# A layer norm's reciprocal root by ScalarE's square root, a reciprocal and one Newton step, in a Macaron block of two expert layers around a Mamba layer

## The reference

```python
x = x + 0.5 * ffn(layernorm(x))     # 64 experts, top 3, hidden 512, capacity 64 per expert
x = x + mamba(layernorm(x))         # projection, 4-tap convolution, selective scan over 16 states
x = x + 0.5 * ffn(layernorm(x))

def layernorm(x, eps=1e-5):
    m, v = mean(x), var(x)
    return (x - m) / sqrt(v + eps)
```

## Time and profile before

| | us |
|---|---|
| timed runs (three) | 800.65, 801.97, 798.1 |
| median | 800.65 |
| span of the profiled execution, first to last instruction | 795.9 |
| device time of the profiled execution | not among the times shown |
| TensorE busy in the span | 685.0 (86%) |
| VectorE busy | 607.8 (76%), 1042 instructions |
| ScalarE busy | 442.2 (56%), 925 instructions |
| GpSimd busy | 490.3 (62%) |

### The profile page before, as it was taken

One profiled execution on the slowest core, in us unless ns is written; L12 is line 12 of the kernel. 1 busy time (PEld: TensorE's weight loads), 2 busy tenths in 40 slices (PEclk: granted clock), 3 DMA queues, 4 the chain that ended last, 5 costly groups with the idle time before them and its releaser, 6 DMA issues. The chain is left out here.

```text
span 795.9 us, 27862 instructions
## 1 busy us (share of the span) xinstructions
PE 685.0 (86%) x11782; PEld 420.8 (53%) x11782; DVE 607.8 (76%) x1042; ACT 442.2 (56%) x925; POOL 490.3 (62%) x308
## 2 busy tenths in 40 slices
PE   6539999978968999899998989999989439999957
PEld 2524556548644445464554655464546334556547
DVE  7993555536698999899999999989897974555525
ACT  2301555534678878888897997867523102444420
POOL 3004666520248999989999999999961005666520
PEclk8858999999969999999999999999996758999979
DMA  8997998626354441344445143542008805998538
GB/s 275 397 327 211 376 371 301 195 75 262 92 125 109 124 122 36 104 108 138 108 123 120 45 129 78 138 108 57 3 3 293 342 1 168 363 382 276 167 121 318
DMA packets 86087, 141.08 MB, mean 177 GB/s; under 512 B 8340, under 2 KB 33566, under 8 KB 84689
## 3 DMA queue, kind: packets, MB, share of 16 engines
q1 hardware_dynamic: 81552, 126.99, 51.0%
q0 software_dynamic: 4416, 12.39, 4.3%
HBM read 112.02 MB, written 27.57 MB: 175 GB/s over the span
## 5 line engine op out<-in xcount | busy, mean ns | idle before, releaser
L1343 POOL TENSOR_TENSOR BIG<-BIG,R 128x1024 f32<-128x1024 f32 x127 | 305.6, 2435 | 18.5 <-DVE BIG L1266 13.8
L1266 DVE TENSOR_TENSOR_SCAN BIG<-BIG,ps 128x1024 f32<-128x1024 f32 x128 | 285.9, 2270 | 18.4 <-PE ps L896 17.7
L896 PE MATMUL ps<-BIG,stack 64*32 64x128 f32 x8192 | 153.7, 281 | 26.4 <-DVE BIG L1266 21.7
L896 PEld LDWEIGHTS ps<-BIG,stack 64*32 64x32 f32 x8192 | 118.5, 108 | 99.1 <-DVE BIG L1266 66.8
L741 POOL DMA_INDIRECT R<-xn_dram,tok_idx x64 | 65.2, 1019 | 91.1 <-DVE row_idx L674 71.3
L755 POOL DMA_INDIRECT y_dram<-BIG,row_idx x64 | 64.7, 1010 | 64.5 <-DVE BIG L698 57.0
L683 DVE COPY BIG<-ps 128x512 f32<-128x512 f32 x64 | 44.3, 691 | 70.3 <-PE ps L518 70.3
L390 ACT ACTIVATE BIG<-BIG 128x512 f32<-128x512 f32 x64 | 40.4, 631 | 97.1 <-DVE BIG L690 97.1
L1140 ACT ACTIVATE BIG<-R,An 128x510 f32<-128x510 f32 x128 | 84.1, 708 | 5.0 <-DVE BIG L1266 4.9
L1140 ACT ACTIVATE BIG<-BIG,An 128x510 f32<-128x510 f32 x128 | 83.7, 708 | 0.2
L918 PE MATMUL ps<-BIG,fold 128*32 128x512 f32 x512 | 68.8, 611 | 0.0
(11 more groups left out here) (173 smaller groups left out, 1018.9 us busy)
## 6 DMA issues: line engine op xcount, KB each, us to landing
BIG<-in_L_ffn_w SPq DMA_DIRECT2D x120, 512.0 KB, 5.8
BIG<-y_dram SPq DMA_DIRECT2D x18, 512.0 KB, 9.3
BIG<-dt_dram SPq DMA_DIRECT2D x32, 256.0 KB, 4.2
R<-c_dram SPq DMA_DIRECT2D x32, 256.0 KB, 7.2
R<-dt_dram SPq DMA_DIRECT2D x32, 256.0 KB, 5.0
y_dram<-zeros SPq DMA_DIRECT2D x3, 2048.0 KB, 16.2
y_dram<-zeros SPq DMA_DIRECT2D x6, 1024.0 KB, 8.3
xn_dram<-R POOLq DMA_DIRECT2D x2, 2048.0 KB, 11.2
```

The costliest lines, as they stand in the source:

```text
L896: last = nc.tensor.matmul(ps[CW * slot:CW * slot + CW, 2 * (st % 2) + b, :] .rearrange("p (g s k) -> p k g s", g=2, k=4)[:, k], dT[q % 2][ ...
L1266: nc.vector.tensor_tensor_scan(state[st % 3], dA[:, st % 6].rearrange("p b g t -> p (b g t)"), ps[:, u:u + 2, :].rearrange("p b n -> p (b ...
L1343: nc.gpsimd.tensor_tensor(prod[st % RP], state[st % 3].rearrange("p (b g t) -> p b g t", b=2, g=2), Cf[q % 2][:, 2 * gp:2 * gp + 2].rearra ...
```

## The change

The four places outside the scan (first expert stage, tiles 0 to 3 and 4 to 7 of the Mamba stage, second expert stage) get `root_vector` and `root_scalar` in place of `inverse_root`: VectorE adds eps, ScalarE takes the square root, VectorE the reciprocal, and one Newton step and nmr follow. So rstd is raised six times, not thirteen, and a new semaphore, root, tells VectorE that the square root is there. The 24 tiles ahead of the scan keep the old way, since ScalarE's table is another one there. In ScalarE's queue the second square root of the Mamba stage stands between normalise(0) and xt_copy(0). The square root's table set is loaded by hand at ScalarE's start, at the start of the Mamba stage and ahead of the last x_copy. To have a semaphore left for root, b2's transfer is counted on w2's semaphore, and mm2's wait for b2 goes into the one for w2.

```diff
--- before.py
+++ after.py
@@ -90,7 +90,8 @@
-STAT_TOTALS = dict(stats=NI, meanvar=NI, rstd=13)
+STAT_TOTALS = dict(stats=NI, meanvar=NI, rstd=6, root=1)
+NEWTON = 13
 LN_TOTALS = dict(normed=24, normed_act=8, transposed=8, xT=8)
 MOE_TOTALS = dict(logits=5, m8=NI, ix8=NI, ixf=1, mdiff=1, gexp=1, gs=3, V=K, marks=2, mask=2, before=1, running=1,
                   prefix=4, picked=7, W=K, place=K, halves=1, gathered_codes=3, code=1, decode=8, xn_stored=16,
@@ -256,6 +257,29 @@
             step(nc.vector.scalar_tensor_tensor(out=nmr[:, i0:i1], in0=mv[:, i0:i1, 0], scalar=-1.0, in1=r,
                                                 op0=ALU.mult, op1=ALU.mult))
+        def root_vector(e, S, i0, i1, n, m):
+
+            def step(instruction):
+                nonlocal n
+                n += 1
+                instruction.then_inc(S("rstd"), 1)
+                e.wait_ge(*S.at("rstd", n))
+
+            v, y, z, r = rs[:, 0, i0:i1], rs[:, 1, i0:i1], rs[:, 2, i0:i1], rstd[:, i0:i1]
+            step(nc.vector.tensor_scalar(v, mv[:, i0:i1, 1], EPS, None, ALU.add))
+            e.wait_ge(*S.at("root", m + 1))
+            step(nc.vector.reciprocal(r, z))
+            step(nc.vector.tensor_tensor(y, r, r, ALU.mult))
+            step(nc.vector.scalar_tensor_tensor(out=z, in0=y, scalar=-0.5, in1=v, op0=ALU.mult, op1=ALU.mult))
+            step(nc.vector.scalar_tensor_tensor(out=r, in0=z, scalar=1.5, in1=r, op0=ALU.add, op1=ALU.mult))
+            step(nc.vector.scalar_tensor_tensor(out=nmr[:, i0:i1], in0=mv[:, i0:i1, 0], scalar=-1.0, in1=r,
+                                                op0=ALU.mult, op1=ALU.mult))
+
+        def root_scalar(e, S, i0, i1, n):
+
+            e.wait_ge(*S.at("rstd", n + 1))
+            nc.scalar.activation(rs[:, 2, i0:i1], rs[:, 0, i0:i1], ACT.Sqrt).then_inc(S("root"), 1)
+
         def ln_stats(e, S, g0, g1, before_stats=None):
             for g in range(g0, g1 + 1):
                 for i in range(4 * g, 4 * g + 4) if g < g1 else ():
@@ -269,7 +293,7 @@
         def ln_vector(e, S, g0, before_stats=None):
             ln_stats(e, S, g0, 8, before_stats)
             e.wait_ge(*S.at("meanvar", NI))
-            inverse_root(e, S, 0, NI, 0)
+            root_vector(e, S, 0, NI, 0, 0)
         def ln_normalise(e, S):
             for i in range(NI):
@@ -279,6 +303,7 @@
         def ln_scalar(e, S, ST):
+            root_scalar(e, ST, 0, NI, 0)
             e.wait_ge(*ST.at("rstd", STAT_TOTALS["rstd"]))
             for i in range(3, NI, 4):
                 nc.scalar.activation(XN[:, i, :], X[:, i, :], ACT.Identity, bias=nmr[:, i:i + 1],
@@ -309,7 +334,7 @@
                 b = RING + EARLY.index(s)
                 return b, G(f"{name}_{b}"), 16 * (f + 1)
             loads = ROUNDS - (s in EARLY)
-            return s, G(f"{name}_{s}"), 16 * (loads * f + r + 1)
+            return s, G(f"{name}_{s}"), 16 * (loads * f + r + 1) + (16 * (ROUNDS * f + r + 1) if name == "w2" else 0)
         def moe_sync(e, S, f):
             def load_w1(r, s):
@@ -323,7 +348,7 @@
                             w2v[bass.ds(RING * r + s, 1)].rearrange("o p a h -> (o p) a h")).then_inc(loaded, 16)
             def load_b2(r, s):
-                e.dma_start(b2s[s], b2v[bass.ds(RING * r + s, 1)].rearrange("o w a d -> (o w) a d")).then_inc(G(f"b2_{s}"), 16)
+                e.dma_start(b2s[s], b2v[bass.ds(RING * r + s, 1)].rearrange("o w a d -> (o w) a d")).then_inc(G(f"w2_{s}"), 16)
             def reload_w1(j, s, r):
@@ -533,9 +558,10 @@
                 e.wait_ge(*S.at("hT", j + 1))
                 b, loaded, count = weights("w2", f, r, s)
                 e.wait_ge(loaded, count)
+                if b != s:
+                    e.wait_ge(G(f"w2_{s}"), 16 * (2 * ROUNDS - 1) * (f + 1))
                 if later(j):
                     e.wait_ge(*S.at("yo", j - 1))
-                e.wait_ge(G(f"b2_{s}"), 16 * (ROUNDS * f + r + 1))
                 for a in range(2):
                     nc.tensor.matmul(ps[a * CAP:(a + 1) * CAP, 5 + s % 2, 0:D], ones[0:3, 0:CAP], b2s[s][:, a, :],
                                      start=True, stop=False)
@@ -1041,7 +1067,7 @@
             def normalise(q):
                 wait(e, "t_psum", q)
                 if q < 3:
-                    wait(e, "rstd", STAT_TOTALS["rstd"] * (q + 1))
+                    wait(e, "rstd", (6, 12, 12 + NEWTON)[q])
                 for j in range(4):
                     i = 4 * q + j
                     last = nc.scalar.activation(XNc[:, j, :], X[:, i, :], ACT.Identity, bias=nmr[:, i:i + 1],
@@ -1142,7 +1168,10 @@
                 last.then_inc(M("dA"), 1)
             e.wait_ge(M("pads"), 3)
+            nc.scalar.preload_act_table_set("sqrt_and_others")
+            root_scalar(e, MST, 0, 4, 0)
             normalise(0)
+            root_scalar(e, MST, 4, 8, 6)
             xt_copy(0)
             normalise(1)
             raw_copy(0, 0)
@@ -1279,10 +1309,12 @@
             moe_sum(e, F[0], 0)
             stats(0, 4)
-            statistics(0, 4, 0)
+            wait(e, "meanvar", 4)
+            root_vector(e, MST, 0, 4, 0, 0)
             moe_sum(e, F[0], 1)
             stats(4, 8)
-            statistics(4, 8, STAT_TOTALS["rstd"])
+            wait(e, "meanvar", 8)
+            root_vector(e, MST, 4, 8, 6, 1)
             moe_sum(e, F[0], 2)
             for m in range(6):
                 tap(0, m // 3, m % 3)
@@ -1300,7 +1332,7 @@
             diagonal(0, 0)
             diagonal(0, 1)
             stats(20, NI)
-            statistics(8, NI, 2 * STAT_TOTALS["rstd"])
+            statistics(8, NI, 12)
             wait(e, "pads", 4)
             for q in range(NQ + 1):
                 b, f = q + 1, q + 2
```

## The result

The changed kernel took 792.97 us (median of six runs, 791.06 to 796.65), the kernel before, beside it, 801.09 (six runs). The ratio is 0.9904, 95% interval [0.988, 0.9928]: 8 us faster, where 2.0 were forecast and 795.8 was the lower end of the range. Every ratio in this document is to the kernel before as it ran on the same chip in the same round (medians 799.32 to 801.09 us, 821.83 in one round), with its 95% interval in brackets; it need not be exactly the quotient of two medians.

A forecast was written before the change was run, and what follows sets the result against it. TensorE was taken to fill the expert loops, so only waits for four layer-norm roots outside them counted: 0.4 + 1.6 = 2.0 us off 800.65 gave 798.6 us; full range 795.8 to 801.9, the forecast's own 797.6 to 799.9.

The forecast's parts named there:

- The semaphores: Expert loops: one wait less per expert pair on TensorE, which is busy throughout, was put at 0.
- The roots: The four layer-norm preparations outside the loops: shorter root chains were to save 2.0 us in all, 0.4 plus 1.6.
- One root: Each new chain, first VectorE step to normalise: 1.75 us for 32 columns, 1.53 for four, saving about 1.1 us.
- The rival of costlier hops: Crossings to ScalarE and back cost more, or gate sums set the pace: only 0.9 us saved, 799.8 us; chance 0.17.
- First expert stage: Normalise ahead of the first expert loop: first transposed copy 0.4 us earlier, TensorE being late next; bounds 0 and 1.3.
- Mamba start: Two roots at the Mamba stage's start: second normalise and taps 1.6 us earlier, ScalarE late next; bounds 0.7 and 2.2.
- Second expert stage: Normalise ahead of the second expert loop: nothing gained, 1.15 us saved only lengthens a 6 us wait for TensorE.
- Table loads: ScalarE: four added loads, 1.28 us each, fall in its idle time or waits; cost 0.
- the estimate of 0.7 us: Mamba stage: with the skill's 2.66 us table switch the silu would lose its cover and 0.7 us, leaving 1.3.
- The clock rival: TensorE's clock gives more, ahead of the scan and the second stage's transposes: 796.2 us; chance 0.17.
- The losing rival: Second expert stage's first transposes and logits at half clock cost up to 3.25 us: 801.9 us; chance 0.10.
- First scan at 227.0: Sign in the changed profile: the first scan starts at 227.0 us of the span, some 2 us earlier.

The follow-up runs named there:

- before + 236: The kernel before with 236 empty instructions (472 waits on a long-risen semaphore) added where TensorE idles in the first stages; 797.33 us, ratio 0.995.
- after + 20: The changed kernel with 20 empty instructions (40 waits on a long-risen semaphore) added on TensorE ahead of the Mamba stage's 14 first products; 798.52 us, ratio 0.9968.
- the two worst tried: The changed kernel with 84 and with 148 empty instructions added on TensorE in the first stage; 808.98 us (ratio 1.0098) and 808.54 us (1.0118).

## Why the prediction was wrong

**The semaphores: 0.** This is the step that failed. "The waits are in TensorE's instruction stream, and TensorE was busy for the whole of the loop with the same matmuls: 0" holds for the loop, whose length did not change. But the edit takes 20 instructions out of the stream ahead of the scan, and so moves the scan's code to a place where late packets cost less. The runs show 3.4 us (before + 236 against before) to 5.4 us (after + 20 against after) by the place alone; by the intervals 2 to 6 and 1 to 9. The 3.6 us of "issue" ahead of L896 were there to be read in the profile of before. I read only the stretches that the change touches.

**The roots: 2.0.** With the old place held (after + 20 against before), the change is worth 0.9968, 2.6 us with bounds of 0 and 5. With the new place held (after against before + 236, same chip) it is 797.33 - 793.15 = 4.2 us, by the ratios 3.7 with about 3.5 either way. The sum of the other steps, 2.0, lies within both, but the medians can't tell it from 4; what supports it is the rows.
- *One root.* Forecast 1.75 us for 32 columns and 1.53 for four; measured 15.76 - 13.76 = 2.00, 600.57 - 598.73 = 1.84, and 186.62 - 185.10 = 1.52. The square root was 0.23 us against 0.229 assumed. In the first stage the eps step took 0.34 instead of 0.22. The rival of costlier hops falls: 185.31 + 0.20 = 185.51 to the reciprocal at 185.61 is 0.10 us.
- *First expert stage, 0.4.* The chain began 0.61 us later, by chance of the loads, and the copy came at 19.41 against 19.34: 0.54 us gained, as forecast. In the time to the loop it can't be seen, since that differs by over 6 us between profiles (68.8 to 75.2).
- *Mamba start, 1.6.* The taps came 1.99 us earlier, the x projection 200.10 - 198.11 = 1.99. All steps and the order of who is late next were right; transposes and second normalise each came 0.3 to 0.4 us before their forecast. The second square root ended at 188.94, 0.1 us ahead of the last transpose (189.04): of the 0.5 us of cover that were counted on 0.1 was left.
- *Second expert stage, 0.* The root's 1.06 us (2.90 - 1.84) ended in a wait for TensorE, as said. The stretch was 2.7 us shorter all the same, 2.6 of it the gate bias at a higher clock.
- *Table loads, 0.* Right. The silu's load had 0.55 us of cover left, forecast 0.7. An activation stands 0.01 to 0.02 us behind a load's end in the changed kernel too:

```profile
32.26 1.28 ACT L1431 ACT_TABLE_LOAD   x1
33.55 0.20 ACT L1431 ACTIVATE An<-ps 128x32 f32<-128x32 f32 x1
```

Nor is there a gap ahead of one: the copy ahead of the silu's load ended at 195.15, and the load began at 195.16. The drain that the Trainium skill states ("ScalarE: Activation LUTs", "What ACT_TABLE_LOAD costs") is not in these rows, and the estimate of 0.7 us by it falls.

**The clock rival** was partly right, beside the place: in this pair of profiles it gave about 1.7 us ahead of the scan and 2.6 in the second stage's start. The pause ahead of the dip did shrink (2.43 to 1.44 us), but dips also stayed away where it had not shrunk, so the condition is not shown to be the cause. In the second stage's start the eight profiles with the scan's code at -10 to +16 of its old place took 74.9 to 75.7 us and the nine at -20 71.9 to 75.4; whether the pauses cause that was not isolated. The losing rival (the clock takes back) did not come.

**"First scan at 227.0"** came at 225.4: 2.0 by the roots, the rest by the clock's dip. "Wrong if the scans start earlier by something other than 2 us and the clock rows do not say why": they do say why. The prediction failed in a stretch that it had not put on its list.

## What to carry to other kernels

In a long unrolled stream, the place of the code is a term of the sum: an edit that adds or removes instructions on TensorE moves all code behind it, and here that is worth 15 to 17 us of 800 between the changed kernel's place and the two worst tried (0.9904 against 1.0098 and 1.0118; 14.2 and 9.5 us of it in the scans of the profiles). When a small edit gives more than its rows can hold, look for "issue" inside runs of equal instructions, add empty instructions in an idle place before and after judging it, and credit the edit only with what is left at a fixed place (here 2.6 us at one place and 3.7 at the other, of 8). A trial of a few places is then a tuning step of its own, and the next edit on TensorE can undo its gain.

## What the runs showed of the hardware

- TensorE's instructions come in packets of 256 during the run (90 packets, 1.47 MB; 91 with 236 more), and TensorE can stop for 0.6 to 3.4 us at instruction 214 or 215 modulo 256, without any wait in the program, until 1.2 to 1.7 us after that packet has landed (105 of 113 stops). The Trainium skill, "Trainium Architecture — The Big Picture", section "The software stack", says that the streams are brought into the engines when the program is loaded; by these rows TensorE's 1.48 MB here were not, but came during the run.
- Not every such place costs: in the changed kernel most don't. 256 instructions used up in under 2.6 us always ended in a stop (23 of 23); why some packets start later than others was not found.
- After such a pause the granted clock often fell to its lower level. Dips at the 25th and the 33rd scan step occur only in kernels with pauses in chunks 1 and 2.
- An empty instruction with two waits takes 0.106 us on TensorE (start to start, in before + 236).
